# Two attentions whose q and k arrive turned, split and by transfer, with value products in halves

## The reference, cut to what matters

```python
x = x + _layernorm(_L0_attn_ref(_layernorm(x), w_qkv, w_out))      # layer 0
#   qkv = einsum('bnc,ce->bne', x, w_qkv); q, k, v = heads of 16
#   attn = softmax(einsum('bhnd,bhmd->bhnm', q, k) / sqrt(256)); out = attn @ v @ w_out
x = x + _layernorm(_L0_ffn_ref(_layernorm(x), ...))                 # routed experts, two loops
x = x + _layernorm(_L1_attn_ref(_layernorm(x), ...))                # layer 1
#   Q = x @ q_w.T + q_b and so on; scores = Q K^T / sqrt(16) + slopes * (pos_k - pos_q)
#   where(pos_k <= pos_q, scores, -inf); softmax; @ V; @ o_w.T + o_b
x = x + _layernorm(_L1_ffn_ref(_layernorm(x), ...))                 # balanced experts
```

## Time and profile before

| | us |
|---|---|
| median of 3 runs (lowest, highest) | 3406.16 (3405.43, 3414.36) |
| the profiled execution | 3403.33 |
| its span | 3401.6 |
| qkv0 begins | 0 |
| att0 begins | 109 |
| output projection of layer 0 begins | 1003 |
| qkv1 begins | 1964 |
| att1 begins | 2127 |
| output projection of layer 1 begins | 2818 |

### The profile page before, as it was taken

One profiled execution on the slowest core, in us unless ns is written; L12 is line 12 of the kernel. 1 busy time (PEld: TensorE's weight loads), 2 busy tenths in 40 slices (PEclk: granted clock), 3 DMA queues, 4 the chain that ended last, 5 costly groups with the idle time before them and its releaser, 6 DMA issues. The chain is left out here.

```text
span 3401.6 us, 63393 instructions
## 1 busy us (share of the span) xinstructions
PE 2729.3 (80%) x16332; PEld 1619.0 (48%) x16333; DVE 1966.6 (58%) x4600; ACT 1625.9 (48%) x2553; POOL 959.6 (28%) x1653
## 2 busy tenths in 40 slices
PE   8699999999977449995399959688888887718887
PEld 5333333333324438874388724344444444415554
DVE  3488888888845353335533354576667754556641
ACT  3277777777754433333333334366666663302212
POOL 1411111111126115541155444322222213403333
PEclk9699999999995569995599979799999996759999
DMA  6501010010013102214022166111111104322331
GB/s 168 168 20 24 14 25 19 19 25 13 19 40 113 56 16 69 68 58 149 14 69 68 59 174 183 44 26 25 31 26 30 25 10 121 119 92 70 99 100 61
DMA packets 365685, 215.08 MB, mean 63 GB/s; under 512 B 284782, under 2 KB 345842, under 8 KB 364791
## 3 DMA queue, kind: packets, MB, share of 16 engines
q1 hardware_dynamic: 231224, 106.71, 11.8%
q10 hardware_dynamic: 116416, 54.53, 5.5%
q0 software_dynamic: 17920, 52.46, 4.9%
HBM read 129.20 MB, written 85.98 MB: 63 GB/s over the span
## 5 line engine op out<-in xcount | busy, mean ns | idle before, releaser
L339 ACT ACTIVATE att_pr<-att_S 128x1024 f32<-128x1024 f32 (+1 forms) x896 | 836.1, 941 | 427.5 <-ACTq L346 424.4
L379 DVE TENSOR_REDUCE att_mparts<-att_S 128x2 f32<-128x1024 f32 x640 | 777.1, 1225 | 169.1 <-DVEq L375 165.2
L255 PE MATMUL att_S<-att_qT,att_kT 64*128 64x512 f32 (+3 forms) x1792 | 430.0, 472 | 46.4 <-PEq L250 42.1
L271 PE MATMUL att_OP<-att_pr,att_vn 128*32 128x512 f32 (+3 forms) x3584 | 451.1, 564 | 1.0 <-PEq L265 0.7
L243 PE MATMUL att_S<-att_kT,att_qT 64*128 64x512 f32 (+3 forms) x1792 | 391.0, 430 | 74.1 <-PEq L237 62.7
L255 PEld LDWEIGHTS att_S<-att_qT,att_kT 64*128 64x128 f32 x1792 | 175.0, 184 | 471.9 <-issue 460.7
L179 POOL COPY att_vn<-att_raw 128x256 f32<-128x256 f32 x64 | 25.4, 396 | 1148.6 <-POOLq L178 1148.6
L243 PEld LDWEIGHTS att_S<-att_kT,att_qT 64*128 64x128 f32 x1792 | 188.0, 190 | 173.0 <-issue 167.1
L385 DVE CUSTOM_DVE_ANT_0 att_unused<-att_S,att_mask 128x128 f32<-128x128 f32 (+3 forms) x512 | 228.3, 488 | 69.9 <-DVEq L375 69.9
L1067 POOL DMA_INDIRECT experts_xs<-scaled,ffn_source x144 | 140.2, 974 | 353.2 <-SPq L1060 163.5
L1164 DVE COPY experts_y<-experts_Y 128x256 f32<-128x256 f32 x144 | 61.2, 425 | 223.3 <-DVEq L1163 223.3
(11 more groups left out here) (291 smaller groups left out, 4913.0 us busy)
## 6 DMA issues: line engine op xcount, KB each, us to landing
qkv<-qkv_y ACTq DMA_DIRECT2D x64, 384.0 KB, 3.4
att_raw<-qkv SPq DMA_DIRECT2D x96, 256.0 KB, 3.3
rows<-post_rows ACTq DMA_DIRECT2D x32, 384.0 KB, 2.7
ffn_w<-in_w ACTq DMA_DIRECT2D x12, 1024.0 KB
ao<-att_aon SPq DMA_DIRECT2D x32, 256.0 KB, 2.8
post_at<-ao SPq DMA_DIRECT2D x64, 128.0 KB, 3.1
scaled<-rms_zs SPq DMA_DIRECT2D x64, 128.0 KB, 1.7
rms_rows<-mixed SPq DMA_DIRECT2D x32, 256.0 KB, 3.6
```

Of the source, the lines that this page charges most:

```text
L255: mm=pe.matmul(S[:,b,h,f:512],kT[r,s,kt*128:kt*128+128],qT[r,s,c*512+f:c*512+512],start=True,stop=not diag)
L271: mm=pe.matmul(OP[32*j:32*j+32,f:512],vn[:,s,kt,h,:],pr[:,n%4,h,f:512],start=kt<2,stop=g in last_groups,skip_group_check=True)
L339: nc.scalar.activation(pr[:,n%4,:,f:512],S[:,ring["e",n],:,f:512],ACT.Exp,scale=exp_scale).then_inc(s_free[ring["e",n]],1)
L379: nc.vector.tensor_reduce(mparts[:,s,:,2*qt+half],S[:,b,:,0:width(qt,half)],AX.X,ALU.max).then_inc(end,1)
```

## The change

- Both projections multiply the value columns as before (256 columns a tile), but q and k with the weights as the stationary operand and 512 tokens as the moving one, so that they come out turned: 32 blocks of 128 features by 512 tokens (`features`). ScalarE writes the high part of a block in the reduced-precision format, in qkv1 with the bias added in the same instruction; VectorE writes the rest (`high`, `low`); SP stores both with one transfer in runs of 2 KB (`keep_block`). The bias products of q and k go. Loops are unrolled, stages get longer lags (`lagged`), v's store moves from ScalarE's queue to SP's.
- Attention loads each part straight to its rows of `qT` and `kT`, four sets deep: 14 transfers a couple in att0 (six of 16 rows a head, and a row of zeros), 16 in att1 (six a head, and five position rows a head for q and for k, from SBUF). GpSimd's splitting, TensorE's 16 transposes a couple and ScalarE's four copies go. Products take 49 rows (att0) or 53 (att1) instead of 64.
- A value product is cut into two pieces of 256 queries. One piece stands at the head of every step, three steps after its exponentials' first block (LAG=3), ahead of the step's score product. `evac_o` moves ahead of the exponential of its step, and the first `finish` of a couple from step KEYS0+1 (NS-4) stays at NS-4 (ADD0).

```diff
+                def load_set(b,pair):
+                    s=pair%SETS; done=set_loaded[s]
+                    sp.wait_ge(set_free,1).then_inc(set_free,-1)
+                    for m,T,high,both in ((0,qT,A,A+HD),(1,kT,A+2*HD,A)):
+                        for h in range(2):
+                            to=lambda row,n: T[64*h+row:64*h+row+n,s,:].bitcast(F32)
+                            parts=qk_d[m][:,bass.ds(b*HEADS+2*pair+h,1)].bitcast(F32)
+                            sp.dma_start(to(high,HD),parts[0,0]).then_inc(done,16)
+                            for x in range(2): sp.dma_start(to(both+HD*x,HD),parts[x,0]).then_inc(done,16)
+                            if causal: sp.dma_start(to(0,AUG),augr[AUG*(2*pair+h):AUG*(2*pair+h)+AUG,m,:].bitcast(F32)).then_inc(done,16)
+                            elif m==0: sp.dma_start(to(0,1),zeros[:].bitcast(F32)).then_inc(done,16)
...
+                COUPLES=2*GROUPS
+                def during(b,c,first,last):
+
+                    def later(c): return (b+1,c-COUPLES) if c>=COUPLES else (b,c)
+                    if not (last and c+3>=COUPLES): load_set(*later(c+3))
+                    if c%2==0:
+                        if c>0: store(b*GROUPS+c//2-1)
+                        elif not first: store(b*GROUPS-1)
+                        if not (last and c+2>=COUPLES): load_v(later(c+2)[0],c//2+1 if c+2<COUPLES else 0)
+                    if not (last and c+1>=COUPLES): place(c+1)
+                for c in range(3): load_set(0,c)
+                load_v(0,0)
...
+                def group():
                     pool.wait_ge(rv_loaded,16).then_inc(rv_loaded,-16)
-                    values(0)
+                    values(0); values(1)
+                    pool.drain().then_inc(rv_free,1)
...
-                def fill(s,f,half):
-
-                    if f==1 and half==0: pe.wait_ge(nat_ready[s],1).then_inc(nat_ready[s],-1)
-                    t_bank_read()
-                    for t in range(4):
-                        mm=pe.transpose(TP[:,128*t:128*t+128].bitcast(F32R),(kn,qn)[f][:,s,4*half+t].rearrange("p h w -> p (h w)"),identr[:])
...
+                    if x==0: pe.wait_ge(set_loaded[s],16*LOADS).then_inc(set_loaded[s],-16*LOADS)
...
+                def pv(s,p):
+                    g,part=divmod(p,2)
+                    if p==0: pe.wait_ge(v_ready[s%2],1).then_inc(v_ready[s%2],-1)
                     for h in range(2):
                         for x in range(2):
-                            n=2*g+x; c,kt=steps[n]; f=first_col(c,kt); j=2*h+x
-                            mm=pe.matmul(OP[32*j:32*j+32,f:512],vn[:,s,kt,h,:],pr[:,n%4,h,f:512],start=kt<2,stop=g in last_groups,skip_group_check=True)
-                    if g in last_groups: mm.then_inc(o_full,1)
+                            n=2*g+x; c,kt=steps[n]; f=max(first_col(c,kt),256*part); j=2*h+x
+                            if f<256*part+256: mm=pe.matmul(OP[32*j:32*j+32,f:256*part+256],vn[:,s%2,kt,h,:],pr[:,n%4,h,f:256*part+256],start=kt<2 and part==0,stop=g in last_groups,skip_group_check=True)
+                    if p in last_pieces: mm.then_inc(o_full,1)
...
+                def slot(j,first,count):
+
+                    def set_of(ahead): return (j+ahead)%SETS if 0<=first+j+ahead<count else None
+                    e,prev,m,a=set_of(0),set_of(-1),set_of(1),set_of(2)
                     for n in range(NS):
+                        g=(n-2)//2 if n>1 else GROUPS_PV-1
+                        who=prev if n<2 else e
+                        p=n-LAG
+                        of=e if p>=0 else prev
+                        if of is not None:
+                            if p in (0,2*CHUNK0): o_ready(p,prev)
+                            pv(of,p%NS)
                         if e is not None: qk(e,n)
                         x,ahead=max_at(n)
-                        if m is not None and n==0: t_bank_read()
-                        if a is not None and n==NS-EARLY: t_bank_read()
                         s=a if ahead else m
                         unit=x is not None and s is not None
                         if unit: scores(s,x)
                         if m is not None and n==TURN: turn_max()
-                        if m is not None and n==0: fill(m,0,1)
-                        if m is not None and n==2: t_bank_read(); pe.sem_inc(nat_free[m],1)
-                        if a is not None and n==QUERIES0: fill(a,1,0)
-                        if a is not None and n==KEYS0-1: fill(a,0,0)
-                        if a is not None and n==NS-2: fill(a,1,1)
-                        g=(n-2)//2 if n>1 else GROUPS_PV-1
-                        who=prev if n<2 else e
-                        if who is not None:
-                            if n%2==0 and not unit: exp_read(2*g+1)
-                            if n%2==1:
-                                if g in (0,CHUNK0): o_ready(g,e,prev)
-                                pv(who,g)
+                        if prev is not None and n==2: pe.sem_inc(set_free,1)
+                        if who is not None and n%2==0 and not unit: exp_read(2*g+1)
                         if prev is not None and n==4: finish()
-                        if e is not None and n==KEYS0+1: finish()
-                def o_ready(g,e,prev):
-                    if g==0 and prev is not None: o_read(free_v=prev)
-                    if g==CHUNK0: o_read()
-                fill(0,1,0); fill(0,0,0)
-                t_bank_read()
+                        if e is not None and n==ADD0: finish()
...
-                        if a is not None and n==KEYS0: evac(a,0,0)
-                        if a is not None and n==NS-1: evac(a,1,1)
...
+                        if prev is not None and n==LAG-1: evac_o()
+                        if e is not None and n==O_FULL0: evac_o()
                         if e is not None: act.wait_ge(exp_full,1).then_inc(exp_full,-1)
...
+HB=6
+def block_of(qk_d,q):
+
+    b,g,f=q//TILES,q%TILES//4,q%4
+    return qk_d[f//2][:,b*HEADS+8*(f%2):b*HEADS+8*(f%2)+8,:,512*g:512*g+512].rearrange("x h d q -> (h d) x q").bitcast(F32)
+
+def tile_of(ap,n):
+    return ap[128*n:128*n+128,:]
+
+def lagged(stages):
+
+    for n in range(NT+max(lag for lag,stage in stages)):
+        for lag,stage in stages:
+            if 0<=n-lag<NT: stage(n-lag)
...
+                def features(q):
+                    f=q%4
+                    pe.wait_ge(q_free,1).then_inc(q_free,-1)
+                    for k in range(KC):
+                        mm=pe.matmul(Q[:,q%4],w[:,k,128*f:128*f+128],xT[:,k,q//4%3,:],start=k==0,stop=k==KC-1)
+                    mm.then_inc(q_full,1)
+                lagged(((5,values),(3,turn),(8,features)))
...
+                def high(q):
+                    act.wait_ge(q_full,1).then_inc(q_full,-1); act.wait_ge(hl_stored[q%HB],16).then_inc(hl_stored[q%HB],-16)
+                    nc.scalar.activation(hl[:,q%HB,0],Q[:,q%4],ACT.Copy).then_inc(high_ready,1)
...
+                def low(q):
+                    dve.wait_ge(high_ready,1).then_inc(high_ready,-1)
+                    done(nc.vector.tensor_tensor(hl[:,q%HB,1],Q[:,q%4],hl[:,q%HB,0].bitcast(F32),ALU.subtract))
+                    dve.sem_inc(q_free,1); dve.sem_inc(low_ready,1)
```

More of the change, by code:

```diff
@@ L137, in _ @@
                     for tile,value in zip(held,held_d): sp.dma_start(tile[:],value).then_inc(held_loaded,16)
[L138 to L141, removed]
+                place(0)
+                for c in range(COUPLES): during(0,c,True,False)
+                with sp.Fori(1,BATCH-1) as b:
+                    for c in range(COUPLES): during(b,c,False,False)
+                for c in range(COUPLES): during(BATCH-1,c,False,True)
                 store(BATCH*GROUPS-1)
@@ new lines, in slot, with o_ready @@
+                        if prev is not None and n==4: finish()
+                        if e is not None and n==ADD0: finish()
+                def o_ready(p,prev):
+                    if p==0 and prev is not None: o_read(free_v=prev)
+                    if p==2*CHUNK0: o_read()
+                for x in range(EARLY): scores(0,x)
+                ALL=BATCH*2*GROUPS
+                for j in range(-1,SETS): slot(j,0,ALL)
+                with pe.Fori(1,ALL//SETS-1):
+                    for j in range(SETS): slot(j,SETS,ALL)
@@ L325, in _ @@
+                for j in range(SETS): slot(j,ALL-SETS,ALL)
+                pv((ALL-1)%SETS,NS-3)
                 exp_read(NS-1)
-                pv(1,GROUPS_PV-1)
+                pv((ALL-1)%SETS,NS-2); pv((ALL-1)%SETS,NS-1)
                 o_read()
@@ L608, in attn_post @@
+                for i in range(HB): act.wait_ge(hl_stored[i],16)
 def attn_post(nc,tag,ao,w_d,x_in,ident_d,x_out=None,z=None,bias_d=None,g_d=None,b_d=None,cent_d=None,rows_d=None,scores=None):
@@ L1277, in _ @@
-                done(V.tensor_copy(high[:],bias[:]))
-                done(V.tensor_tensor(low[:],bias[:],high[:].bitcast(F32),ALU.subtract))
-                done(V.tensor_scalar(low[:],low[:],ident[0:2,1:2],None,ALU.mult))
```

(8 more changed lines are left out.)

481 lines of the change are left out of this document (198 added, 283 removed).

## The result

The changed kernel takes **3465.5 us** (median of 4 runs, 3459.5 to 3467.5) against 3405.8 (4 runs, 3400.4 to 3414.4) for the kernel before on the same chip: a ratio of 1.017, 95% interval 1.0145 to 1.0195. It is slower by 60 us, where 3249 was forecast and 3345 was the upper end. The profiled execution took 3464.6 (span 3462.9).

A forecast was written before the change was run, and what follows sets the result against it. Att0 was taken as bound by a latency loop holding the long value product, att1 as nearer TensorE's busy sum. Terms -67-88+4+0+3-9=-157 took 3403.3 to 3246, plus 2.9: 3249 us; own range 3200 to 3300, stated range 3170 to 3345.

The forecast's parts named there:

- The loop of att0: Att0: exp, row-maximum product and value product form a latency loop, 3.23 us per two steps, 2.79 with halved value products.
- Att0's couple, 24.3: Att0: a couple falls from 26.4 to 24.3 us, -67 us over 32 couples.
- Rivals A and B: Attentions: VectorE takes over the ring, 3336 us, chance 0.20; or only the fullest engine counts, 3172 us, chance 0.10.
- Att1's couple, 17.6: Att1: a couple falls from 20.35 to 17.6 us, -88 us over 32 couples.
- The closing transposes' wait of 1.07: Att1: TensorE's 1.07 us wait per couple for PSUM bank TP before the closing transposes goes.
- TensorE's busy sum of 16.4: Att1: TensorE's busy time per couple falls from 17.9 to 16.4 us, less four fills, plus split value products.
- the wait alone, 19.3: Att1: upper bound of the couple, 19.3 us, if only the wait at the closing transposes goes, -34 us.
- Starts: Start of the attentions: att0 +4 us (0 to +21) from loads queued ahead of the first placement, att1 0.
- Row loads: SP's queue: 14 to 16 loads a couple at 0.5 us each, hidden in att1 with 1.9 us to spare.
- D: Score products: two heads no longer run side by side with 49 or 53 rows; 3466 us, chance 0.05.
- Projections: Qkv0: tile 3.0 us, VectorE-bound, +3 us; qkv1: tile 3.6 us instead of 3.89, -9 us.
- C: SP's queue: row loads come late and delay the maximum's placement; slower, 3495 us at 1.1 us a load, chance 0.07.

The follow-up runs named there:

- Run 1: Changed kernel with TensorE's 32 slots of both attentions written out in a row instead of a repeating part of four; 3447.8 us, 1.0101 of the kernel before.
- run 4: Changed kernel with undivided value products, all 512 columns ahead of every second step's score product; 3438.1 us, 1.0082 of the kernel before.
- run 8: Changed kernel with slots in a row, unread transposes in att1 and the output store on ScalarE's queue; 3374.0 us, 0.989 of the kernel before.
- run 2: Changed kernel with 64 rows a head instead of 53 in att1's score and row-maximum products; 3438.6 us, 1.0094 of the kernel before.
- run 7: Changed kernel with slots in a row, unread transposes in att1, and the store issued after 8 of a set's 16 loads; 3442.4 us, 1.0118 of before.
- run 9 without transposes: Changed kernel with slots in a row, store on ScalarE's queue, att1's maxima over at most 256 columns; 3334.8 us, 0.9782 of the kernel before.

## Why the prediction was wrong

- **The loop of att0: right.** 2.79 for two steps, forecast 2.79; 3.22 when the product is undivided again, forecast 3.23.
- **Att0's couple, 24.3: mis-sized.** It takes 24.9, so 32 couples give -48 and not -67. Rivals A and B, which moved the same term, are both off.
- **Between the couples of att0: the step that failed there.** The part on att0 went from one couple straight to 32x(26.4-24.3) and never asked what lies between them. The change doubles the repeating part from two slots to four and the products a slot from 153 to 201; one turn goes from 708 instructions to 1782. Cost: five waits of 3.9 to 4.3 us (20 us) and the slow products after them; the 18 couples between the first score products at 345.0 and 841.5 take 496.5 instead of 449, so **+47** in all. With a first exp 7 us later and some 7 us more, 4 of them behind the last couple's first score product and the rest not assigned, -48+47 makes the +13. Run 1 takes the waits and these falls away, run 4 ties them to the size of the part.
- **Att1's couple, 17.6: wrong.** The closing transposes' wait of 1.07 went, as forecast (2200:2840 of the changed kernel):

```profile
L256 PE MATMUL att_TP<-att_ident,att_ot 128*128 128x128 f32 x240 | 45.7, 321 | 0.0
```

  But of the two terms behind 17.6, TensorE's busy sum of 16.4 and the 1.2 kept for other waits, only the first was right: of the 78.6 us of four couples at full clock (2288.1:2327.2 and 2374.0:2413.5) TensorE is busy 66.8, so 16.7 a couple, and waits 2.9. I had summed TensorE and left VectorE out of att1's loop. With narrow maxima the couple is 18.2, TensorE 370.2/22=16.8 busy and 1.4 of waits; so most of the missing waits, not all, are VectorE's. The value that stood as the upper bound (the wait alone, 19.3) was nearly the truth: 32x0.65=-21.
- **The clock: the term that was missing.** Every duration of the prediction was one at full clock, and nothing in it asked whether the clock would stay there once 16 transposes a couple and a sixth of the rows (53 for 64) were gone. In att1 it did not: the 30 couples between the first score products at 2206.1 and 2849.3 take 643 us, 52 more than at 19.7. With them -20+52, a start 2.6 us later, 3.7 in the first couple and 6.7 behind the last one's first score product make the +45. That idle transposes and a store issued earlier bring 45 us back in att1 (run 8, 691.6, with slots in a row) is shown, and so is that 64 rows alone bring back 30 (run 2); which property of the step the clock looks at is open.
- **Starts: low.** Att0's first exp is 51.2 us into the stage instead of 44.2, where +4 was forecast. The maximum was ready at 150.2; SP was still issuing the expert weights and tables, one issue taking 6.81 us, and the placement's transfer then shared the DMA engines with them (0.98 busy from 159.6 to 167.5):

```profile
149.95 0.27 DVE L367 CAST att_mT<-att_S 16x128 fp32r<-16x128 f32 x1
...
152.68 6.81 SPq L152 DMA_DIRECT2D ffn_marks<-in_marks  x1
...
159.60 1.68 SPq L131 DMA_DIRECT2D att_qT<-att_mT  x2
...
167.56 0.80 PE L231 MATMUL att_S<-att_qT,att_kT 49*128 49x512 f32 x2 [15.74 <-PEq L226]
```

- **Row loads: right.** In the set issued from 2311.75 each of the 12 loads from memory takes 0.32 to 0.45 (single ones elsewhere up to 1.5), the four position rows 0.70 to 0.75, the whole set of 16 takes 8.5 us, 0.53 each against 0.5 forecast; no first product of a slot waits for a placement in the timelines read. D is refuted (pairs stay 0.34 apart); that its sum, 3466, is the measured time is chance.
- **Projections: sign right, sizes off.** A tile of qkv0 takes 3.16 (59.71 to 62.87), not 3.0; one of qkv1 3.26 (2060.46 to 2063.72), near the 3.3 of TensorE alone, and in part longer (2066.98 to 2070.51, 3.53). What the tiles don't explain lies ahead of them: the first wide product starts 20.0 us into the program instead of 11.7 in qkv0 and 48.8 us into the stage instead of 30.8 in qkv1, since a block needs four tiles. The prediction had a shorter ramp in qkv0 and none in qkv1; the 8 us are all of qkv0's loss, and the 18 take back most of what qkv1's faster tiles give.

The error was not in how much work goes, which came out well, but in taking the speed of the work that stays as given. A rival "slower" with a place of its own was there (C and D), with 12% between them; neither was what happened, though C's place is real (run 7).

## What to carry to other kernels

When a change lengthens a repeating part, count the instructions that its engine issues in one turn and look for "issue" idle time at the turn; here 1610 were free and 1782 cost 4 us each time, and the clock with it. When a change takes work off a TensorE that sets the pace, ask what keeps its clock up afterwards, read the granted clock before anything else in the new profile, and try idle work in the waits and an earlier release of the wait ahead of the first slow product. And write the loop of each stage for itself: dividing the long product helped att0 and did nothing in att1, where VectorE's maxima close the loop.

## What was not expected of the hardware

- A turn of TensorE's loop with 1782 instructions stands 3.9 to 4.3 us, one with 1610 shows no wait, and 44 blocks of instructions are fetched in 520 us where the shorter loop fetches 2. Written out in a row, the same instructions never waited, with 36 blocks fetched in those 520 us (run 1): it is the turn that costs, not the fetching.
- The clock fell in att1 with no wait over 1.1 us near the fall:

```profile
2346.82 0.50 PE L231 MATMUL att_S<-att_qT,att_kT 53*128 53x512 f32 x2 [0.28 <-PEq L226]
...
2348.64 0.79 PE L231 MATMUL att_S<-att_qT,att_kT 53*128 53x512 f32 x2 [0.86 <-PEq L226]
...
2350.22 1.07 PE L248 MATMUL att_OP<-att_pr,att_vn 128*32 128x256 f32 x8
```

The product of 2348.64 is already slow. The busy share does not tell the cases apart: 84% held the full clock (run 4, att0), 84 to 86% lost it (33.19 of 39.50 us and 33.65 of 39.10 in the changed att1, measured between the falls), 93% held it (run 9 without transposes). The Trainium skill (TensorE: Matmul & The Clock Gate, A second HAM failure mode: psum-queue depth-cycling) tells of a kernel whose small, frequent waits between groups made the clock swing; the trace of att1 agrees, and that of att0 with undivided products, with three waits of 0.5 to 0.7 us a couple, as many as att1 has over 0.5, does not.
- Fewer rows in the score products (53 for 64) cost clock: 276 us at half clock against 157 with 64 rows and nothing else changed in att1's steps (run 2; the totals of its four executions, 3431.5 to 3449.3, all lie below those of the changed kernel).
